# Second layer of a two-layer model: up tiles, key matrices, last convolution and gates in another order

## The reference, cut to what matters

```
q, k, v = silu(conv4(x @ Wq.T)), silu(conv4(x @ Wk.T)), silu(conv4(x @ Wv.T))   # causal, 4 taps
q, k = l2norm(q), l2norm(k);  beta = sigmoid(x @ Wb.T)
g = -exp(A_log) * softplus(x @ Wa.T + dt_bias)
def step(S, q_t, k_t, v_t, g_t, b_t):
    S = S * exp(g_t);  u = b_t * (v_t - k_t @ S);  S = S + outer(k_t, u);  return S, (q_t * scale) @ S
```

## Time and profile before

| | |
|---|---|
| median of 3 runs | 1563.21 us (1561.12 to 1566.44) |
| the profiled execution | 1562.83 us, its span 1561.0 us |
| PE busy | 1375.8 us, 88% |
| DVE busy | 1145.0 us, 73% |
| ACT busy | 716.7 us, 46% |
| POOL busy | 489.0 us, 31% |

### The profile page before, as it was taken

How to read it: one execution, slowest core, us unless ns; L and a number is a source line. 1 busy time by engine, 2 the same in 40 slices (tenths; PEclk the granted TensorE clock), 3 DMA queues, 4 the chain that set the end, 5 groups by cost and what they waited for, 6 DMA issues and landing times. The chain is left out here.

```text
span 1561.0 us, 24324 instructions
## 1 busy us (share of the span) xinstructions
PE 1375.8 (88%) x8972; PEld 665.3 (43%) x8972; DVE 1145.0 (73%) x1911; ACT 716.7 (46%) x1257; POOL 489.0 (31%) x412
## 2 busy tenths in 40 slices
PE   3777799999999999999989878988899889998887
PEld 1222233333333333333345456553575436654374
DVE  6778887778877887888646866669667795676854
ACT  2454366556655665566564322543135422264121
POOL 1237941012201220122126412254213533145231
PEclk9989899999999999999999999999999999999999
DMA  4511000010001000102620130010300203002111
GB/s 146 195 55 48 1 8 7 15 35 15 8 15 35 15 8 15 35 14 98 233 77 21 31 81 16 27 42 11 82 28 14 52 5 78 35 7 52 30 27 41
DMA packets 79573, 68.51 MB, mean 44 GB/s; under 512 B 45952, under 2 KB 67168, under 8 KB 76896
## 3 DMA queue, kind: packets, MB, share of 16 engines
q1 hardware_dynamic: 79456, 66.96, 14.6%
HBM read 44.87 MB, written 17.87 MB: 40 GB/s over the span
## 5 line engine op out<-in xcount | busy, mean ns | idle before, releaser
L577 DVE TENSOR_REDUCE mS<-bank 128x1 f16<-128x512 f32 x512 | 328.9, 685 | 105.0 <-PE bank L1045 103.1
L866 ACT ACTIVATE probs<-bank 128x512 f16<-128x512 f32 x512 | 277.1, 594 | 165.9 <-PE bank L1052 165.8
L1099 PE MATMUL bank<-rows,both 128*128 128x512 f16 x1024 | 243.0, 380 | 0.9 <-DVE th L606 0.7
L393 POOL TENSOR_TENSOR h<-th,h 128x512 f16<-128x512 f32 x58 | 68.1, 1174 | 244.5 <-ACT h L837 244.5
L1099 PEld LDWEIGHTS bank<-rows,both 128*128 128x128 f16 x1024 | 91.4, 98 | 124.1 <-issue 16.8
L2038 PE MATMUL fbank<-both,hid 128*128 128x512 f16 x512 | 121.4, 400 | 25.9 <-DVE hid L1585 25.9
L2022 PE MATMUL fbank<-rows,both 128*128 128x512 f16 x512 | 119.9, 389 | 4.7 <-ACT hid L1843 4.7
L1045 PE MATMUL bank<-qk 32*128 32x512 f16 x512 | 101.2, 391 | 25.4 <-DVE mS L577 6.9
L2006 PE MATMUL abank<-rows,both 128*128 128x512 f16 (+1 forms) x480 | 114.0, 390 | 4.7 <-PEq L149 4.7
L1052 PE MATMUL bank<-qv,qk 32*128 32x512 f16 x512 | 100.0, 387 | 0.0
L1113 PE MATMUL bank<-dn,h 128*128 128x512 f16 x256 | 98.7, 386 | 0.0
(11 more groups left out here) (283 smaller groups left out, 2650.5 us busy)
## 6 DMA issues: line engine op xcount, KB each, us to landing
h<-in_ug SPq DMA_DIRECT2D x8, 1024.0 KB, 5.1
lt_scratch<-big SPq DMA_DIRECT2D x16, 384.0 KB, 2.7
dn<-in_down SPq DMA_DIRECT2D x2, 2048.0 KB, 9.3
x_scratch<-th SPq DMA_DIRECT2D x16, 256.0 KB, 2.3
res<-x_scratch SPq DMA_DIRECT2D x16, 256.0 KB, 3.5
out_x<-res SPq DMA_DIRECT2D x16, 256.0 KB, 2.0
both<-in_w SPq DMA_DIRECT2D x2, 1548.0 KB, 10.3
t_scratch<-tok SPq DMA_DIRECT2D x8, 384.0 KB, 3.6
```

Source lines behind the costliest of these rows:

```text
L393: pool.tensor_tensor(h16(ft, 1), row32, h16(ft, 0), ALU.subtract).then_inc(S["row_lo"], 1)
L577: v.tensor_reduce(mS[:, u % 2, qt, 32 * j + DH:32 * j + DH + 1], SA[n % 2][:, :], AX.X, ALU.max).then_inc(S["max_done"], 1)
L866: a.activation(probs[:, n % (2 * G), :], SB[n % 2][:, :], ACT.Exp, scale=float(DH) ** -0.5).then_inc(S["p_ready"], 1)
L1099: mm = pe.matmul(GB[n % 2][:, :], w[:, kt, col:col + P], xnb(b, kt), start=r == 0, stop=r == 2 * KT - 1)
```

## The change

On PE all 16 up tiles stand behind the projections: the first two between the last matrices, the others behind them. The products come as KK0, KQ0, KK1, KQ1, KK2, KK3, KQ2, KQ3. POOL and ACT take their parts of the hidden tiles later in the same way, and POOL's `k_norms` (L1465) comes ahead of them. On DVE `conv(7)` goes behind the matrices KQ0, `silu(7)`, `conv(8)` and `silu(8)` behind the substitution, and `scale_down(1)` into its second half. The float32 relu tiles 8 to 15 use two rows of `yT` in place of `r32` and `ct`, which the late convolutions still hold. Waits for the last silu are added ahead of the residual loads (SP), of the first down tanh (ACT) and of the first transposes of k and v (PE).

```
+PAIRS = (("KK", 0), ("KQ", 0), ("KK", 1), ("KQ", 1), ("KK", 2), ("KK", 3), ("KQ", 2), ("KQ", 3))
...
-            return spare[ht % 2] if ht < SPARE else (r32, ct)[ht % 2][:, :]
+            return spare[ht % 2] if ht < SPARE else yT[:, ht % 2, :]
...
+                sp.wait_ge(S["sil_r"], (b + 1) * NM)
                 load_residual(0)
...
                 square(0)
-                hidden(b, 0)
                 square(1)
                 spread(0)
                 spread(1)
                 square(2)
-                hidden(b, 1)
                 square(3)
                 mask(0)
                 square(4)
                 mask(1)
-                hidden(b, 2)
                 square(5)
                 spread(2)
                 spread(3)
-                hidden(b, 3)
                 mask(2)
-                hidden(b, 4)
                 mask(3)
+                k_norms()
...
-                for ht in range(5, HT):
+                for ht in range(HT):
                     hidden(b, ht)
-                k_norms()
...
                 for m in range(3, 7):
                     conv(m)
                     silu(m - 1)
-                conv(7)
...
                     for i in range(0, HB, SLICE):
                         w = i + SLICE
+                        if i == 2 * SLICE:
+                            scale_down(1)
...
-                matrices(0)
+                matrices("KK", 0)
                 silu(6)
-                matrices(1)
-                matrices(2)
-                matrices(3)
-                conv(8)
-                silu(7)
-                silu(8)
+                matrices("KQ", 0)
+                conv(7)
+                for nm, tt in PAIRS[2:]:
+                    matrices(nm, tt)
...
                 invert_blocks()
+                silu(7)
+                conv(8)
+                silu(8)
...
                 second_gate(0)
-                scale_down(1)
                 second_gate(1)
...
                 pre_tile(2)
-                up_tile(0)
                 pre_tile(3)
...
                 pairs("KK", 2, MT)
+                pairs("KK", 3, MT)
+                up_tile(0)
                 pairs("KQ", 2, 0)
-                pairs("KK", 3, MT)
+                up_tile(1)
                 pairs("KQ", 3, 0)
-                for ht in range(6, HT):
+                for ht in range(2, HT):
```

More of the change, by code:

```diff
@@ L1199, in bank_order @@
         a += [(b, "DT", 2, 0), (b, "DT", 2, 1), (b, "sT"), (b, "DT", 3, 0), (b, "DT", 3, 1)]
-        for tt in range(TT):
-            v += [(b, "KK", tt, 0), (b, "KK", tt, 1), (b, "KQ", tt, 0), (b, "KQ", tt, 1)]
+        v += [(b, nm, tt, hf) for nm, tt in PAIRS for hf in range(2)]
         for tt in range(TT + 1):
@@ L1645, in _, with matrices @@
                 v.tensor_scalar(sn5[:, :, :], sn, rowm[:, 0:1], None, ALU.mult).then_inc(S["snm_r"], 1)
[L1647 to L1653, removed]
+                def matrices(nm, tt):
+                    dst = (LT if nm == "KK" else BT)[tt]
+                    for hf in range(2):
+                        v.wait_ge(S["GTm_r"], (b * TT + tt) * 2 + hf + 1)
+                        v.tensor_tensor(dst[:, hf:LH:2, :], mats(take(nm, tt, hf)), GT[tt % 2][:, hf:LH:2, :],
+                                        ALU.mult).then_inc(S["v_took"], 1)
                 def invert_blocks():
@@ L1895, in _ @@
                 tanh_conv(1)
-                hidden(0)
                 evict_pre(3)
@@ L1910, in _ @@
                 tanh_conv(3)
-                hidden(1)
                 evict_pre(5)
@@ L2158, in _ @@
                 differences(3)
-                up_tile(5)
                 pairs("KK", 2, MT)
+                pairs("KK", 3, MT)
+                up_tile(0)
                 pairs("KQ", 2, 0)
-                pairs("KK", 3, MT)
+                up_tile(1)
                 pairs("KQ", 3, 0)
-                for ht in range(6, HT):
+                for ht in range(2, HT):
                     up_tile(ht)
```

27 lines of the change are left out of this document (9 added, 18 removed).

## The result

The changed kernel takes 1576.4 us (median of 8 runs, 1570.9 to 1579.6), the one before 1563.0 us beside it. The ratio is 1.0086, 95% interval 1.0068 to 1.0104: it is slower by 13.4 us, where 17.6 us less were forecast. That is outside the stated range of 1533 to 1557, and above every rival's time (1568 the slowest). The profiled span of after is 1574.9 us, 13.9 more than before.

The account below looks back on a forecast made before the run. Each batch was taken as bound by the time to the last key matrix, the transfers and DVE's substitution; -5.3 - 3.1 + 3.4 + 0.6 = -4.4 us a batch, -17.6 for four, gave 1545.5 us, range 1533 to 1557.

Parts of the forecast that it names:

- Term 1: DVE's path from conv(2) to the first key matrix: 5.3 us a batch shorter, bounds -7.3 to -3.5.
- Term 2: First to last key matrix: 3.1 us a batch shorter, bounds -5.2 to -1.3.
- Term 3: Substitution on DVE: 4.0 us a batch longer, +3.4 from five more POOL hidden operations, +0.6 from scale_down(1).
- the port costs its full price: POOL's hidden operations hold DVE products for their full 1.16 us: +1.2 us a batch, 1568 us; chance 0.08.
- Costed at nothing: Late silu, conv(8), tanh and gates behind the substitution: 7.3 us, covered by 10.0 us of transfers and POOL's diagonal.
- The first rival: PE becomes the bound at scale_down(1) in the substitution: gain 2 us a batch instead of 4.4, 1555 us; chance 0.18.

Follow-up runs that it names:

- experiment 2: Changed kernel with thrown-away matmuls on PE: 14 ahead of the last sums of squares, 8 ahead of KQ1, 16 ahead of X5; 1540.2 us.
- Experiment 11: The kernel of experiment 2 with POOL's subtraction for the hidden tiles replaced by a write of zeros; 1540.6 us.
- experiment 10: Changed kernel, nothing thrown away: up tiles 0 and 1 ahead of the last squares, 2 ahead of KQ1, both down-tile scalings late in the substitution; 1543.2 us.
- experiment 1: Changed kernel with 16 thrown-away matmuls behind the last down tile, ahead of X5; 1558.2 us.

## Why the prediction was wrong

**Term 1 was right in its sum, in part by luck:** -5.3 forecast, -5.6 measured (last batch -5.4, where its parts can be read). The waits of 2.80 and 1.17 us ahead of conv(5) and conv(6) were taken as gone and fell to 1.07 and 0.42; in all about 9.5 us went off the path instead of 11.4. Onto it came about 4.2 instead of 6.1: conv(5) took 3.75 us and not 4.6, and the spreads hardly held the small norms. The two misses of 1.9 us cancel.

**Term 2 failed:** -3.1 forecast, +1.5 measured, and -2.5 when PE is kept busy (experiment 2). The step that failed was to take every product, projected tile and difference at its duration in the earlier trace rows while the same sum gave PE new idle time: 3.28 us ahead of the last sums, 2.64 ahead of KQ1. The durations of before belong to the clock of before.

**Term 3 was near:** +4.0 forecast, +3.1 measured. In the last batch the small products went from 11.8 us to 15.2, the +3.4 of the forecast. But that batch was the best of before: the other three had 12.8 to 13.1 us (8 POOL operations beside the products, not 7), so the mean rise is 2.5. One batch times four overstated it. Experiment 11 prices the POOL operations: 8.5 us for 13 of them, 0.66 each, under the 0.75 of the forecast and well under 1.16. So the rival "the port costs its full price", the only one that forecast a slower kernel, had the sign right and the mechanism wrong.

**"Costed at nothing" was right for what it named.** Both gates end at 1493.8 in the last batch and X5 starts at 1496.9, 3.1 us of cover where I had 2.7. It failed in what it did not name, and what the sum therefore had at nothing: the same edit that moves scale_down(1) forward moves the pause of PE ahead of the recurrence, which then starts at the lower clock. Measured +4.4 us a batch, and 22 us for that line alone in the kernel before.

**The first rival held the cause and had the wrong size.** It named PE's slower pace behind idle time, among the projections and ahead of X5, but took 1 us for the start of the recurrence and two drops of 1.3 us each for the rest, and expected them to bite through scale_down(1), which never waited in the changed kernel. The price was 4.4 and 4.1 us a batch. It was counted as 2.4 us less gain (2 instead of 4.4); the true sum is -5.6 + 1.5 + 3.1 + 4.4 = +3.4, times four 13.6 us, against 13.9 in the spans. What spoke against it, the up tiles at full pace behind 1.56 us of waiting in the earlier trace rows, was a pause shorter than the ones that the change makes.

The Trainium skill (TensorE: Matmul & The Clock Gate, "HAM oscillation — how this bites in real kernels") says that waits between bursts of matmuls let the clock drop, so that each burst starts slowly. The trace agrees, 0.50 of full clock behind 4.32 us of idle time; I had not weighed the rule.

## What to carry to other kernels

Work of another branch that PE does in the waits of the critical branch holds its clock; it is not in the way just because it stands ahead of the product one waits for. Before moving it, list each idle stretch of PE that the new order makes and what stands right behind it on the path, and cost that at 1.6 to 1.9 times its duration, as measured here (2.76 to 4.33 us, 1.56 to 2.93). If there is a pause, put real work there, or leave the pause ahead of work that is off the path (experiment 10 does both: 1543.2 us, 1.2% faster than before), or, where no work is left, matmuls into a bank that is about to be overwritten (experiment 2: 1540.2 us, 1.4% faster; only experiment 11, which leaves out a part of the result, is as fast).

## What the hardware showed that was not expected

The way from X5 to the first state product, against the time that PE stood still right ahead of X5, in all batches of the profiled executions of before, after and the twelve experiments:

| idle ahead of X5 | batches | X5 to first state product |
|---|---|---|
| 0.08 to 1.8 us | 30 | 7.5 us in 26, 8.6 to 8.7 in 4 |
| 2.4 to 4.5 us | 26 | 9.2 to 10.6 us |

Between them nothing was measured. With the short products here (64x64, with waits in between) the low clock lasted through the first step and in 17 of the 26 batches of the second row into the second: K1 then came 13.7 to 15.2 us after the first state product instead of 11.4. The four exceptions in the first row are not explained, and in two of them K1 came late too (14.3 us). So a short pause right ahead of X5 makes the full clock likely, not certain. Single runs of one kernel scattered with the clock: in experiment 1, 1552.3 us had a mean granted clock of 0.972 and 1570.6 us one of 0.957.
